# Routed experts of a four-layer kernel: each F32 product as three F32R products of split operands

## The reference

```
logits = ht @ gate_w
top_vals, top_idx = jax.lax.top_k(logits, K)          # K = 2 of E = 8
gates = jax.nn.softmax(top_vals, axis=-1)
for e in range(E):
    we = jnp.sum(gates * (top_idx == e), axis=-1)
    ye = jax.nn.silu(ht @ w1[e]) * (ht @ w3[e]) @ w2[e]   # 256 -> 896 -> 256
    out = out + we[:, None] * ye
```

## Time and profile before

| | us |
|---|---|
| median of 3 runs | 2934.72 |
| lowest and highest run | 2931.69, 2934.95 |
| span of the profiled execution | 2931.5 |
| PE busy | 2457.6 (84%) |
| DVE busy | 1531.5 (52%) |
| ACT busy | 1078.7 (37%) |
| POOL busy | 659.7 (23%) |

### The profile page before, as it was taken

How to read it: one execution, slowest core, us unless ns; L and a number is a source line. 1 busy time by engine, 2 the same in 40 slices (tenths; PEclk the granted TensorE clock), 3 DMA queues, 4 the chain that set the end, 5 groups by cost and what they waited for, 6 DMA issues and landing times. The chain is left out here.

```text
span 2931.5 us, 40280 instructions
## 1 busy us (share of the span) xinstructions
PE 2457.6 (84%) x11935; PEld 1585.6 (54%) x11996; DVE 1531.5 (52%) x3474; ACT 1078.7 (37%) x2278; POOL 659.7 (23%) x661
## 2 busy tenths in 40 slices
PE   6699996499999569999995776999997818999990
PEld 3233334399999312222214554677777817888880
DVE  6444424788888764444416886677774421112224
ACT  3133331244444113333332454788884201222210
POOL 0000001255555100000001554444440040000005
PEclk9699997599999769999997988999998858999995
DMA  3622200000000161212101223222225414444432
GB/s 109 93 45 53 47 15 6 22 29 21 21 21 7 61 101 29 43 33 39 29 0 61 91 104 128 73 97 98 102 94 205 143 69 172 179 179 179 179 138 90
DMA packets 119097, 234.92 MB, mean 80 GB/s; under 512 B 15216, under 2 KB 85744, under 8 KB 111856
## 3 DMA queue, kind: packets, MB, share of 16 engines
q1 hardware_dynamic: 115952, 225.64, 24.8%
q0 software_dynamic: 3072, 8.39, 0.9%
HBM read 165.30 MB, written 68.68 MB: 80 GB/s over the span
## 5 line engine op out<-in xcount | busy, mean ns | idle before, releaser
L808 DVE TENSOR_REDUCE c_att_nmax<-bank 128x1 f32<-128x512 f32 x256 | 175.2, 691 | 227.0 <-PE bank L667 200.9
L1901 PE MATMUL bank<-e_moe_hT,e_moe_w 128*128 128x256 f32 x1288 | 284.6, 382 | 5.8 <-DMA e_moe_w<-in_e_w 5.8
L696 PE MATMUL bank<-c_att_probs,c_att_vq 128*32 128x512 f32 x512 | 268.1, 606 | 2.3 <-issue 0.4
L1901 PEld LDWEIGHTS bank<-e_moe_hT,e_moe_w 128*128 128x128 f32 x1288 | 246.6, 192 | 40.2 <-DMA e_moe_w<-in_e_w 6.2
L754 ACT ACTIVATE c_att_probs<-bank 128x512 f32<-128x512 f32 x256 | 152.2, 598 | 272.5 <-PE bank L688 270.7
L1338 DVE SCALAR_TENSOR_TENSOR b_acc<-bank,b_gates,b_acc 128x256 f32<-128x256 f32 x512 | 212.4, 477 | 41.4 <-PE bank L1253 41.4
L546 POOL TENSOR_SCALAR d_att_probs<-d_att_probs,d_att_rinv 128x128 f32<-128x128 f32 (+2 forms) x192 | 178.2, 928 | 218.0 <-DVE d_att_rinv L557 218.0
L808 DVE TENSOR_REDUCE a_att_nmax<-bank 128x1 f32<-128x128 f32 (+3 forms) x256 | 124.9, 491 | 184.8 <-PE bank L670 173.1
L1306 POOL TENSOR_TENSOR b_moe_act_low<-b_moe_act,b_moe_act_high 128x512 fp32r<-128x512 f32 x136 | 176.8, 1300 | 176.7 <-ACT b_moe_act_high L1283 176.7
L1946 DVE TENSOR_TENSOR e_moe_act<-bank,e_moe_silu 128x256 f32<-128x256 f32 x161 | 68.4, 425 | 273.2 <-ACT e_moe_silu L1930 273.2
L436 PE MATMUL bank<-d_att_k,d_att_q 128*128 128x128 f32 (+3 forms) x512 | 188.5, 451 | 18.0 <-DMA d_att_k<-k_dram 17.8
(11 more groups left out here) (329 smaller groups left out, 5479.6 us busy)
## 6 DMA issues: line engine op xcount, KB each, us to landing
e_moe_w<-in_e_w SPq DMA_DIRECT2D x23, 2688.0 KB, 10.0
q_dram<-d_in_rot SPq DMA_DIRECT2D x16, 1024.0 KB, 3.9
d_att_q<-q_dram SPq DMA_DIRECT2D x16, 1024.0 KB, 5.0
o_dram<-d_att_o SPq DMA_DIRECT2D x64, 256.0 KB, 2.0
d_out_oT<-o_dram SPq DMA_DIRECT2D x16, 1024.0 KB, 5.6
b_moe_w<-in_b_w SPq DMA_DIRECT2D x17, 512.0 KB, 3.3
a_att_q<-q_parts SPq DMA_DIRECT2D x128, 64.0 KB, 3.1
a_att_k<-k_parts SPq DMA_DIRECT2D x128, 64.0 KB, 3.2
```

What stands on the lines that cost most here:

```text
L696: mm = nc.tensor.matmul(obank[h // 4 % 2][VW * u:VW * (u + 1), lo:S], vq[h // 4][:, u, kt, :], probs[h % 2][:, kt, lo:S], start=(kt == 0), ...
L808: nc.vector.tensor_reduce(nmax[:, h % 8, qt:qt + 1], rbank[qt % 2][:, 0:keys(qt)], AX.X, ALU.max, negate=True).then_inc(max_ready, 1)
L1901: mm = nc.tensor.matmul(ph[f % 4][:, i * SLOTS:(i + 1) * SLOTS], up[:, k, i, f * P:(f + 1) * P], hT[s][:, k, :], start=(k == 0), stop=(k = ...
```

## The change

`swiglu_blocks` alone is changed. Each of the operands `ws`, `hT` and `act` gets a high and a low half in F32R, and each F32 product becomes three F32R products: high x high, high x low, low x high, summed in the same PSUM bank. ScalarE rounds the high halves of weights and activations. GpSimd subtracts the weights' high halves from the weights, in 7 chunks of 768 columns (`CH`), and VectorE does the same for the activations and for `hT`. The weights of block j + 1 are split while block j is computed, one chunk behind each silu. SP now waits for the low halves of a block's weights (`w_low`) and not for the block's result before it loads over them, and its stores are issued four blocks late instead of two. TensorE's up part waits for all seven low chunks of its weights, its down part for the low half of each activation chunk. `act` becomes a ring of four.

The core of the diff:

```diff
+                def reload(j, s):
+                    sp.wait_ge(w_low, FC1 * (j - 1))
+                    sp.wait_ge(tr_done, j - 1)
+                    load(j, s)
...
-                with sp.Fori(1, BLOCKS // 2) as m:
+                reload(2, 0)
+                reload(3, 1)
+                with sp.Fori(2, BLOCKS // 2) as m:
                     for s in range(2):
-                        sp.wait_ge(y_done, 2 * m + (s - 1))
-                        load(2 * m + s, s)
-                        store(2 * m + (s - 2), s)
+                        reload(2 * m + s, s)
+                        store(2 * m + (s - 4), s)
...
-                    pe.wait_ge(hT_ready, 2 * j + 2)
-                    pe.wait_ge(w_in[s], 16 * m + 16)
+                    pe.wait_ge(hT_low, KT * j + KT)
+                    pe.wait_ge(w_low, FC1 * j + FC1)
...
                             for k in range(KT):
-                                mm = nc.tensor.matmul(ph[f % 4][:, i * SLOTS:(i + 1) * SLOTS], up[:, k, i, f * P:(f + 1) * P],
-                                                      hT[s][:, k, :], start=(k == 0), stop=(k == KT - 1))
+                                for x, y in PRODUCTS:
+                                    mm = nc.tensor.matmul(ph[f % 4][:, i * SLOTS:(i + 1) * SLOTS], up[x][:, k, i, f * P:(f + 1) * P],
+                                                          hT[s][y][:, k, :], start=(n == 0), stop=(n == 3 * KT - 1))
+                                    n += 1
...
                             if i == 0:
-                                pe.wait_ge(act_ready, FC1 * j + (f + 1))
-                            mm = nc.tensor.matmul(py[s][:, i * D:(i + 1) * D], act[:, f, i * P:(i + 1) * P], down[:, f, :],
-                                                  start=(f == 0), stop=(f == FC1 - 1))
+                                pe.wait_ge(act_low, FC1 * j + (f + 1))
+                            for n, (x, y) in enumerate(PRODUCTS):
+                                mm = nc.tensor.matmul(py[s][:, i * D:(i + 1) * D], ap[x][:, f, i * P:(i + 1) * P], down[y][:, f, :],
+                                                      start=(f == 0 and n == 0), stop=(f == FC1 - 1 and n == 2))
...
+                def high_weights(s, f):
+                    nc.scalar.copy(wp[s][0][:, chunk[f]], ws[s][:, chunk[f]]).then_inc(w_high, 1)
+
+                def high_act(j, f):
+                    a.wait_ge(act_ready, FC1 * j + (f + 1))
+                    if f == 0:
+                        a.wait_ge(y_done, j)
+                    nc.scalar.copy(ap[0][:, f, :], act[:, f % 4, :]).then_inc(act_high, 1)
+
+                def block_of(m, s, following):
+                    j = 2 * m + s
                     for f in range(FC1):
                         a.wait_ge(up_done, FC1 * j + (f + 1))
                         nc.scalar.activation(silu[:, f % 4, :], ph[f % 4][:, 0:SLOTS], ACT.Silu).then_inc(silu_ready, 1)
+                        if following:
+                            if f == 0:
+                                a.wait_ge(w_in[1 - s], 16 * (m + s) + 16)
+                                a.wait_ge(y_done, j)
+                            high_weights(1 - s, f)
+                        if f:
+                            high_act(j, f - 1)
+                    high_act(j, FC1 - 1)
+                    if following:
+                        keep_hT(j + 1, 1 - s)
...
+            @block.gpsimd
+            def _(g):
+                def low_weights(j, s, f):
+                    g.wait_ge(w_high, FC1 * j + (f + 1))
+                    g.tensor_tensor(wp[s][1][:, chunk[f]], ws[s][:, chunk[f]], wp[s][0][:, chunk[f]], ALU.subtract).then_inc(w_low, 1)
...
             @block.vector
             def _(v):
-                def experts(m, s):
+                def low_act(j, f):
+                    v.wait_ge(act_high, FC1 * j + (f + 1))
+                    nc.vector.tensor_tensor(ap[1][:, f, :], act[:, f % 4, :], ap[0][:, f, :], ALU.subtract).then_inc(act_low, 1)
+
+                def low_hT(j, s):
+                    for k in range(KT):
+                        v.wait_ge(hT_high, KT * j + (k + 1))
+                        nc.vector.scalar_tensor_tensor(out=hT[s][1][:, k, :], in0=tr[k][:, 0:SLOTS], scalar=col[:, k:k + 1],
+                                                       in1=hT[s][0][:, k, :], op0=ALU.mult, op1=ALU.subtract).then_inc(hT_low, 1)
...
                     for f in range(FC1):
                         v.wait_ge(silu_ready, FC1 * j + (f + 1))
-                        nc.vector.tensor_tensor(act[:, f, :], ph[f % 4][:, SLOTS:], silu[:, f % 4, :], ALU.mult).then_inc(act_ready, 1)
...
+                        nc.vector.tensor_tensor(act[:, f % 4, :], ph[f % 4][:, SLOTS:], silu[:, f % 4, :], ALU.mult).then_inc(act_ready, 1)
+                        if f:
+                            low_act(j, f - 1)
+                    low_act(j, FC1 - 1)
+                    if following:
+                        low_hT(j + 1, 1 - s)
+                    keep_y(m, s)
```

More of the change, by code:

```diff
@@ L1831, in swiglu_blocks, with sb @@
     WU, WF = KT * 2 * F1, KT * 2 * F1 + FC1 * D
+    CH = WF // FC1
     NI = SLOTS // P
     LAST = BLOCKS - 1
+    PRODUCTS = [(0, 0), (0, 1), (1, 0)]
     assert BLOCKS % 2 == 1
     with ExitStack() as ctx:
-        def sb(n, shape):
-            return ctx.enter_context(nc.sbuf_tensor(f"{name}_{n}", shape, F32))
+        def sb(n, shape, dt=F32):
+            return ctx.enter_context(nc.sbuf_tensor(f"{name}_{n}", shape, dt))
         def sem(n):
@@ L1842, in swiglu_blocks @@
         ws = [sb(f"w{s}", [P, WF]) for s in range(2)]
+        wp = [[sb(f"w{s}_{part}", [P, WF], F32R) for part in ("high", "low")] for s in range(2)]
         hs = [sb(f"h{s}", [P, NI, D]) for s in range(2)]
-        hT = [sb(f"hT{s}", [P, KT, SLOTS]) for s in range(2)]
+        hT = [[sb(f"hT{s}_{part}", [P, KT, SLOTS], F32R) for part in ("high", "low")] for s in range(2)]
         ys = [sb(f"y{s}", [P, NI, D]) for s in range(2)]
         col = sb("col", [P, KT])
-        silu, act = sb("silu", [P, 4, SLOTS]), sb("act", [P, FC1, SLOTS])
+        silu, act = sb("silu", [P, 4, SLOTS]), sb("act", [P, 4, SLOTS])
+        ap = [sb(f"act_{part}", [P, FC1, SLOTS], F32R) for part in ("high", "low")]
         w_in, h_in, y_free = ([sem(f"{n}{s}") for s in range(2)] for n in ("w_in", "h_in", "y_free"))
-        col_in, tr_done, hT_ready, up_done, silu_ready, act_ready, y_done, y_ready = (
-            sem(n) for n in ("col_in", "tr", "hT", "up", "silu", "act", "y_done", "y_ready"))
-        ph, py, tr = c.bank[0:4], c.bank[4:6], c.bank[6]
+        col_in, tr_done, hT_high, hT_low, up_done, silu_ready, act_ready, act_high, act_low, w_high, w_low, y_done, y_ready = (
+            sem(n) for n in ("col_in", "tr", "hT_high", "hT_low", "up", "silu", "act", "act_high", "act_low", "w_high", "w_low",
+                             "y_done", "y_ready"))
+        ph, py, tr = c.bank[0:4], c.bank[4:6], c.bank[6:8]
+        chunk = [slice(f * CH, (f + 1) * CH) for f in range(FC1)]
         block = nc.Block()
@@ L1869, in _ @@
                 load(1, 1)
-                with sp.Fori(1, BLOCKS // 2) as m:
+                reload(2, 0)
+                reload(3, 1)
+                with sp.Fori(2, BLOCKS // 2) as m:
                     for s in range(2):
-                        sp.wait_ge(y_done, 2 * m + (s - 1))
-                        load(2 * m + s, s)
-                        store(2 * m + (s - 2), s)
-                sp.wait_ge(y_done, LAST - 1)
-                load(LAST, 0)
-                for j in range(LAST - 2, LAST + 1):
+                        reload(2 * m + s, s)
+                        store(2 * m + (s - 4), s)
+                reload(LAST, 0)
+                for j in range(LAST - 4, LAST + 1):
                     store(j, j % 2)
@@ L1885, in turn @@
                     pe.wait_ge(h_in[s], 16 * m + 16)
+                    pe.wait_ge(hT_low, KT * (2 * m + s))
                     for k in range(KT):
                         for i in range(NI):
-                            mm = nc.tensor.transpose(tr[:, k * SLOTS + i * P:k * SLOTS + (i + 1) * P], hs[s][:, i, k * P:(k + 1) * P], c.ident[:, :])
+                            mm = nc.tensor.transpose(tr[k][:, i * P:(i + 1) * P], hs[s][:, i, k * P:(k + 1) * P], c.ident[:, :])
                     mm.then_inc(tr_done, 1)
@@ L1892, in experts @@
                     j = 2 * m + s
-                    up, down = ws[s][:, 0:WU].rearrange("p (k i f) -> p k i f", k=KT, i=2), ws[s][:, WU:].rearrange("p (f n) -> p f n", n=D)
-                    pe.wait_ge(hT_ready, 2 * j + 2)
-                    pe.wait_ge(w_in[s], 16 * m + 16)
+                    up = [t[:, 0:WU].rearrange("p (k i f) -> p k i f", k=KT, i=2) for t in wp[s]]
+                    down = [t[:, WU:].rearrange("p (f n) -> p f n", n=D) for t in wp[s]]
+                    pe.wait_ge(hT_low, KT * j + KT)
+                    pe.wait_ge(w_low, FC1 * j + FC1)
```

(34 more changed lines are left out.)

4 lines of the change are left out of this document (2 added, 2 removed).

## The result

| | us |
|---|---|
| before, median of 4 runs | 2934.29 (2931.69 to 2934.95) |
| changed kernel, median of 4 runs | 3010.27 (3008.55 to 3011.43) |
| ratio | 1.0261, 95% interval 1.0247 to 1.0276 |
| span of the profiled execution | 3008.4 (before 2931.5) |

The changed kernel is 76 us slower. It was forecast at 2996.7 us, in a range of 2950 to 3035.

What follows compares the result with a forecast made beforehand. TensorE bounds the kernel in each block. The loop's 14.0 + (20.1 + 2.8) + 21 x 20.1 + 15.1 = 474.1 us is +44.4; with 17.6 for the clock, +62.0 on 2934.7 gives 2996.7 us, range 2950 to 3035.

Steps and rivals of the forecast that it cites:

- second bound: In a block, GpSimd's seven subtractions alone would set the pace: 16.0 us per block, still a gain of 2.6 us.
- the holding: VectorE's activation low halves and GpSimd's subtractions each wait for the other's whole instruction less 0.13 us: 2.02 us per pair.
- GpSimd's pace and the lead ahead of it: In a block, GpSimd's first subtraction starts at 2.86 us; each takes 1.86 us, seven 13.0 us.
- TensorE's tail: In down, 24 products, 2.88 us, stand behind the seventh low half at 17.1: 20.1 us per block with the signal.
- The clock: TensorE's clock falls between sparse triples late in a block: 0.8 us per block taken, 17.6 for 22 blocks.
- The start: Before the first block, TensorE waits 14.0 us for the split; the block after it costs 2.8 more at low clock.
- the 20 to 21 that I gave as a sign: Sign in the loop's timeline that the forecast holds: blocks are 20 to 21 us apart.
- (1): Rival: no holding, as VectorE's low halves don't meet GpSimd; 16.0 us per block, 2889 us; chance 0.08.
- (2): Rival: holding on one side, VectorE waits and GpSimd loses nothing; 19.1 us per block, 2957 us; chance 0.10.
- (3): Rival: VectorE and GpSimd hold each other, but TensorE's clock stays up; 2979 us; chance 0.26.
- (4): The forecast itself: both engines hold, with a clock cost of 0.4 to 1.2 us per block; 2988 to 3006; chance 0.30.
- (5): Rival: a clock cost of 1.7 to 3.0 us per block; 3016 to 3045 us; chance 0.20.

Runs made afterwards that it cites:

- experiment 1: Changed kernel with the product of silu and gate written back into its PSUM bank, not SBUF, so VectorE's low half reads one SBUF input: 2881.0 us.
- experiment 2: Changed kernel with 30 more F32R products per block, of results nobody reads, ahead of TensorE's waits for the fifth to seventh low half: 2976.1 us.
- experiment 8: Changed kernel with each low half of the activations made by two VectorE instructions of 128 columns, not one of 256: 3023.7 us.

## Why the prediction was right, and by how much it was off

- **What bounds the kernel.** Right: TensorE in each block, and only there could the change gain. The F32R products came at 0.12 us, and the last block took 15.2 us (15.1 forecast). Right too, as a second bound: by itself GpSimd would give blocks of 16.0 us; without the holding they are 15.67 (experiment 1).
- **GpSimd's pace and the lead ahead of it.** Forecast: first subtraction at 2.86, 1.86 us each alone. Measured: 2.81, and 1854 ns in experiment 1. One subtraction starts a little before the record of the one ahead of it ends, so seven alone take 12.71 us and not 13.0.
- **The holding, both ways.** Forecast: a pair in 2.02 us, the seventh subtraction at 16.8 and the seventh low half at 17.1. Measured in the block at 2643.25: 13.71 us for seven, 16.5 and 16.8 us; GpSimd is busy for 65% of the window, as forecast. The 0.13 us of start-up that overlap carried over from the earlier trace rows to other sizes. The Trainium skill's rule ("SBUF — State Buffer", "Who interferes with whom") holds on both of its sides: held with two SBUF inputs (1410 ns), free with one (423 ns in experiment 1).
- **TensorE's tail.** Forecast: 24 products behind the last low half, 20.1 us per block at the full clock. Measured: 19.90, experiment 2.
- **The clock: the term that was mis-sized.** Forecast 0.8 us per block, out of 0 to 4.3: a fall of 3.4 us, half of it in the wait. Measured 21.62 - 19.90 = 1.72. Both sizes were off. The low stretches are longer, 13.66 us in three blocks or 4.6 each, and nine tenths of them (12.16 us) lie on the chain, because the clock falls about when the last wait ends. The price was a little lower than the half that I took: a product costs 0.213 us in place of 0.12, so a low us loses 0.44 us. 12.16 / 3 x 0.44 = 1.78 us, by the traces alone. The row of the shorter fall, all of it on the chain, would have given 1.7 as well, but by luck. I had an argument for each side and took a middle.
- **The start.** Forecast 14.0 us of split that nothing hides, measured 13.3 from the first copy to the first product; the first block with its low clock 23.57 us against 22.9 + 0.8.
- **The sum.** 13.3 + 23.57 + 21 x 21.62 + 15.2 = 506.1 us, against 429.7: +76.4, which is the difference of the spans, 76.9, but for 0.5. The forecast had +62.0. Of the 14 us between them 21 x 0.72 = 15.1 are blocks, less 0.7 at the start and the end. The blocks are 21.6 us apart, past the 20 to 21 that I gave as a sign.
- **The rivals.** (1), no holding, is what experiment 1 is: 2881 us against 2889 forecast. (2) fell by GpSimd's 1984 ns against 1854 without the holding. (3), the clock stays up since no pause is long, fell by the windows above: no pause in the triples was over 1.34 us. (4) had the mechanism, but its interval, 2988 to 3006, ends below the result. The time lies between (4) and (5), and with 1.72 us per block it is (5)'s cost of the clock, on blocks that were 0.2 us shorter than I had them. I gave (5) less than (4).

## What to carry to other kernels

Before elementwise work is split between VectorE and GpSimd, look for the pair of a VectorE instruction with two SBUF inputs and a GpSimd instruction beside it: in this kernel each such pair cost the rest of the instruction under way, and keeping one operand in PSUM removed it. Where TensorE has to wait for an operand again and again, put as few products as possible behind the last wait: here the 24 behind it cost 2.9 us, and 1.7 more because the clock fell in the waits. What nothing hides, such as the first block's split, goes to the engine that does it fastest.

## What the runs showed of the hardware that was not expected

- TensorE's granted clock fell in a stretch in which it was never idle for more than 1.34 us: two or three triples of 0.35 us, one each 1.95 us. The fall then lasted 3.4 us in two blocks of three and 6.8 us in the third. The shortest pause that I had read ahead of a fall was 2.66 us. Products whose results nobody reads, put into the pauses, kept it at 1.00 and made the kernel 34 us faster.
- When both VectorE and GpSimd have an instruction ready, they take strict turns (experiment 8), whichever is shorter. I had known only one half of it, VectorE ahead of GpSimd's next one, from one row.
